# Two normalizations applied on GpSimd in the attention stages, and one wait ahead of the coefficient sum

## What is computed

```python
x = x + 0.5 * ffn(layernorm(x), gate_w, expert_w)
x = x + attn(layernorm(x), Wq, bq, Wk, bk, Wv, bv, Wo, bo)
x = x + 0.5 * ffn(layernorm(x), gate_w, expert_w)

# layernorm: (x - mean) / sqrt(var + 1e-5) over the 1024 features
# ffn:  logits = x @ gate_w.T; top 2 of 8 experts, softmax over the two;
#       out = sum over experts of weight[n, e] * (x @ expert_w[e].T)   (all 8 experts are computed)
# attn: q = f(x Wq + bq), k = f(x Wk + bk), f(z) = exp(-z*z/2); v = x Wv + bv
#       coeff = sum over a head's 64 features of q*k, per token; out = (coeff * v) Wo + bo
```

## Time and profile before

| | us |
|---|---|
| runs shown (2) | 3063.6 and 3078.4, median 3071.0 |
| the profiled execution | 3060.3 |
| its span on the slowest core, first to last instruction | 3058.8 |
| spans of the 8 cores | 3048.6 to 3058.8 |
| one pair of tiles in the steady state | about 355 |

### The profile page before, as it was taken

One profiled execution on the slowest core, in us unless ns is written; L12 is line 12 of the kernel. 1 busy time (PEld: TensorE's weight loads), 2 busy tenths in 40 slices (PEclk: granted clock), 3 DMA queues, 4 the chain that ended last, 5 costly groups with the idle time before them and its releaser, 6 DMA issues.

```text
span 3058.8 us, 58132 instructions; the slowest of 8 cores (3048.6 to 3058.8 us)
## 1 busy us (share of the span) xinstructions
PE 2618.4 (86%) x22240; PEld 2073.3 (68%) x22240; DVE 897.0 (29%) x1920; ACT 526.1 (17%) x1201; POOL 1196.9 (39%) x1059
## 2 busy tenths in 40 slices
PE   0029979998899979998799978999799988999799
PEld 0018757786678857786578856787577865788568
DVE  0012442214411352224432144122522144221530
ACT  0011231103111121112211031111211023110310
POOL 1015215560355405552155603553055512555045
PEclk9999999999999999999999999999999999999999
DMA  9960230104101040103201041011401032010500
GB/s 150 186 174 1 87 108 29 56 1 138 56 29 56 31 164 1 71 14 105 90 29 56 1 153 42 29 56 53 141 16 69 1 111 84 28 43 1 172 22 29
DMA packets 48316, 205.21 MB, mean 67 GB/s; under 512 B 6040, under 2 KB 6040, under 8 KB 42928
## 3 DMA queue, kind: packets, MB, share of 16 engines
q1 hardware_dynamic: 43920, 176.20, 16.8%
q0 software_dynamic: 4128, 25.30, 5.2%
HBM read 201.61 MB, written 25.17 MB: 74 GB/s over the span
## 4 chain that ended last, share of the span: by engine, by line
PE 73%; DVE 10%; DMA 8%; issue 3%; ACT 2%; DVEq 2%; POOL 1%; ACTq 0%; SPq 0%; POOLq 0%
PE P L434 56%; PE P L570 4%; PE P L502 3%; DMA Wexp<-w_exp 3%; DVE yecB L299 2%; PE P L512 2%; PE P L610 2%; DMA Wab<-w_attn 2%; DMA Wab<-w_attn_bf 2%; PE P L252 2%; PE P L224 1%; DVEq L118 1%; DVE yecA L299 1%; DVE SAB L302 1%; DMA w_attn_bf<-Wab 1%
## 5 line engine op out<-in xcount | busy, mean ns | idle before, releaser
L424 POOL TENSOR_TENSOR yecA<-SAA,SCA 128x512 bf16<-128x512 bf16 x512 | 589.5, 1155 | 1301.6 <-ACT SCA L399 873.7
L434 PE MATMUL P<-yecA,Wexp 128*128 128x256 bf16 x8192 | 934.3, 273 | 10.7 <-POOL yecA L424 8.9
L434 PE MATMUL P<-yecB,Wexp 128*128 128x256 bf16 x8192 | 921.1, 273 | 0.0
L434 PEld LDWEIGHTS P<-yecA,Wexp 128*128 128x128 bf16 x8192 | 784.5, 98 | 142.1 <-issue 51.4
L434 PEld LDWEIGHTS P<-yecB,Wexp 128*128 128x128 bf16 x8192 | 790.1, 98 | 118.1 <-issue 27.4
L424 POOL TENSOR_TENSOR yecB<-SAB,SCB 128x512 bf16<-128x512 bf16 x512 | 591.6, 1159 | 386.2 <-PE P L434 380.7
L452 DVE TENSOR_TENSOR XT<-XT,P 128x512 f32<-128x512 f32 x128 | 79.4, 682 | 652.0 <-PE P L434 652.0
L224 PE MATMUL P<-SAA,onescol 128*1 128x256 bf16 x192 | 25.8, 278 | 203.5 <-DVE SAA L211 202.9
L224 PEld LDWEIGHTS P<-SAA,onescol 128*1 128x1 bf16 x192 | 14.5, 84 | 213.0 <-issue 209.1
L502 PE MATMUL P<-SAB,Wab 128*128 128x256 bf16 x512 | 78.6, 305 | 53.6 <-DVE SAB L302 35.2
L244 ACT ACTIVATE yecA<-SAA 128x512 bf16<-128x512 bf16 x96 | 60.4, 629 | 311.8 <-PE P L252 184.4
(11 more groups left out here) (129 smaller groups left out, 1968.9 us busy)
## 6 DMA issues: line engine op xcount, KB each, us to landing
Wab<-w_attn_bf SPq DMA_DIRECT2D x256, 512.0 KB, 4.2
Wexp<-w_exp POOLq DMA_DIRECT2D x8, 2048.0 KB, 49.3
XT<-x_in SPq DMA_DIRECT2D x16, 1024.0 KB, 5.6
x_out<-XT SPq DMA_DIRECT2D x16, 1024.0 KB, 4.2
Wab<-w_attn POOLq DMA_DIRECT2D x16, 512.0 KB, 10.2
w_attn_bf<-Wab SPq DMA_DIRECT2D x16, 512.0 KB, 8.8
id<-c_id POOLq DMA_DIRECT2D x1, 32.0 KB, 2.5
IND<-c_ind POOLq DMA_DIRECT2D x1, 32.0 KB, 2.2
```

What stands on the lines that cost most here:

```text
L424: yd = inc("gp", lambda g, _c=c0, _e=e, _p=pp: g.tensor_mul(yec[:, _p * 2 * T:(_p + 1) * 2 * T].rearrange("p (h n) -> p h n", h=2), sa[:, ...
L434: fn = lambda tt, _e=e, _c=c, _dj=dj, _p=pp, _h=half, _bk=bank, _lo=lo: tt.matmul(_bk[:, _lo:_lo + T], Wexp[:, ((_e * NCH + _c) * D + _dj ...
```

## The change

With `use_gp` set, the four subtracts and four multiplies of the normalization go to POOL's list in place of DVE's, with POOL's semaphore `gq`, POOL's wait for `mrbb`, and POOL's drains. `y_pair` and `y_done` now hold the name of the semaphore beside its value, and the gate and the attention stage wait for that (`wait_tok`). Apart from this, the eight waits of PE for `qk_done[c]`, one ahead of each coefficient matmul, are replaced by one wait for `qk_done[7]` ahead of all eight. No instruction is added or taken away on the engines otherwise, and the steps keep their places.

```diff
@@ ln_chain
-        wait("ve", "se", bcv_done)
+        wait("ve" if not use_gp else "gp", "se", bcv_done)
+        ap_eng, ap_sem = ("gp", "gq") if use_gp else ("ve", "ve")
...
-            op("ve", lambda v, _s=sv, _y=yv: v.tensor_sub(
+            op(ap_eng, lambda E, _s=sv, _y=yv: E.tensor_sub(
                 _y, _s, St.mrbb[:, :].unsqueeze(1).to_broadcast([128, 2, T])))
-            drain("ve")
-            y_pair[cp] = inc("ve", lambda v, _s=sv, _y=yv: v.tensor_mul(
-                _s, _y, St.rbb[:, :].unsqueeze(1).to_broadcast([128, 2, T])), "ve")
-            drain("ve")
+            drain(ap_eng)
+            y_pair[cp] = (ap_sem, inc(ap_eng, lambda E, _s=sv, _y=yv: E.tensor_mul(
+                _s, _y, St.rbb[:, :].unsqueeze(1).to_broadcast([128, 2, T])), ap_sem))
+            drain(ap_eng)
@@ gate_chain
-                wait("pe", "ve", y_pair[c // 2])
+                wait_tok("pe", y_pair[c // 2])
@@ attn_phase
-        wait("pe", "ve", y_done)
+        wait_tok("pe", y_done)
...
+        wait("pe", "ve", qk_done[7])
         coeff_done = None
         for c in range(NCH):
-            wait("pe", "ve", qk_done[c])
             fn = lambda tt, _c=c: tt.matmul(
                 B2[0:16, 0:T], IND[:, _c * 16:(_c + 1) * 16], sc[:, _c * T:(_c + 1) * T],
```

## The result

The changed kernel is slower: its ratio to the kernel before is 1.0289, with a 95% interval of 1.0269 to 1.0310. On 3064 us, what the kernel before takes as a rule in the same series, that is 89 us, where 75 were forecast. Lines from L294 on are one higher than before: L300 and L303 are the subtract and the multiply (before L299, L302), L319 the gate, L503 the query product, L552 the coefficient sum.

A forecast was written before the change was run, and what follows sets the result against it. PE, busy 86%, was taken as the bound, with normalizations on its path. 34.8 + 27.8 + 12.3 = 75 us on 3060.3 gives 3135, on the median 3071.0 gives 3146; it took 3141 us, range 3114 to 3178.

The forecast's parts named there:

- The hole: Between the attention stages PE waits for SAB; POOL ends 4.35 us later than DVE did, 34.8 us in the run.
- The period: Time from one drained POOL normalization operation's start to the next: 1.275 us, with a gap of 0.12.
- The bounds of 1.11 and 1.745: Limits in us per POOL operation: no drain cost from below, 0.59 us idle before each from above.
- The gate: Gate matmuls in the second attention stage wait for SAA; POOL ends 3.48 us later, 27.8 us in the run.
- I add nothing: Longer PE waits between the stages and at L318 meet an already fallen clock, so no extra clock cost.
- Part 2: One wait ahead of all eight coefficient matmuls delays seven of them: 0.77 us a stage, 12.3 us in the run.
- the third rival: Clock falls at the coefficient sum as PE's wait grows to about 2.2 us: 42 us more, 3183; chance 0.07.
- The prediction's own sign of being wrong: Windows after L551, the coefficient sum, showing a clock of 0.5.
- The sum: Whole run: 34.8 + 27.8 + 12.3 = 75 us.
- POOL's floor: POOL's normalization operations start 1.11 us apart despite drains: 56 us in all, 3122, within 2%; chance 0.16.
- POOL at 0.83 us an operation: Fast POOL normalization operations, twice DVE's 0.42 us: would cost 20 us in the run, 3086; chance 0.03.
- The dear drain: POOL idles 0.59 us before each normalization operation, as after PE's release: 53 us more, 3194; chance 0.06.

The follow-up runs named there:

- the runs of either place alone: Kernel before with only LN 2 of B on POOL, ratio 1.0128; kernel before with only LN 3 of A on POOL, ratio 1.0117.
- the fillers: Matmuls nobody reads, run while PE waits: changed kernel with 76 between the stages and 12 ahead of the one wait, 1.0216; kernel before with 36 between the stages, 0.9937.
- The runs with fillers: Unread matmuls ahead of the single qk_done[7] wait: 12 there and 76 between the stages in the changed kernel, 1.0216; seven in the kernel before with that wait, 1.0003.
- Part 2 measured alone, the one wait alone: Kernel before with the single wait for qk_done[7] and every normalization on DVE: ratio 1.0046, 14 us.
- a crowded schedule: Kernel before with LN 2 advanced at every yield from the fifth, both normalizations on POOL: 1.0129; LN 3 advanced too: 1.0032 on POOL, 1.0150 on DVE.
- the one wait with fillers: Kernel before with the single wait for qk_done[7], all on DVE, and seven unread matmuls ahead of that wait: ratio 1.0003.
- all was on DVE one step early: Kernel before, all on DVE, eight waits, LN 2 begun from the second yield and LN 3 from the first: ratio 1.0030.
- LN 2 early on POOL: Kernel before with both normalizations on POOL, eight waits, LN 2 of B advanced at every yield from the fifth: ratio 1.0129.
- LN 3 alone on POOL: Kernel before with only LN 3 of A, carried by the second attention stage, on POOL: ratio 1.0117, 36 us.

## Why the prediction was right, and where it was off

- **The hole.** Forecast 4.35 us more a pair; measured 4.50 in a steady pair (8.89 against 4.39) and 4.98 as a mean of the whole stretch. POOL's start, 0.14 us after ACT, and PE's, 0.36 after POOL, came as forecast. The period was 1.30 us, not 1.275: the gap behind a drain is 0.14 to 0.16 instead of the 0.12 taken. The bounds of 1.11 and 1.745 held it, and it lies where ACT's hand-over pointed.
- **POOL's first use** was not in the sum. In the first pair the first multiply began 2.69 us late, and the hole was 11.44 us. It costs some 2.6 us in the run.
- **The gate.** Forecast 3.48 us; from mrbb to the sixth value block it was 3.65, and the part of the stage grew by 3.67. The difference is the longer period, seven times 0.025. That everything behind the gate moves with it, and that DVE's freedom gives nothing back, is borne out by the runs of either place alone.
- **Clock behind the hole and the gate.** "I add nothing" was right for the hole: the fillers took 2.04 us out of the changed kernel and 2.18 out of the one before. At the gate it came out by a balance that the prediction had not seen. The three value blocks behind the gate take 4.68 us on average instead of 4.33, and the three ahead of it 3.35 instead of 3.96.
- **Part 2, the step that failed, within a sum that held.** The step was that the seven matmuls cost their 0.77 us and the clock nothing, with the third rival, a fall of the clock at the sum, kept apart at 0.07. Together the two stages' parts up to the output blocks grew by 1.82 us in the first (forecast 0.77). The runs with fillers show 0.80 and 0.83 us of it without the clock's part, so the first term was right and about 1 us of clock was missing in the first stage. The rival named the mechanism but mis-sized it. It put 2.6 us on every one of 16 places, from the long hole; behind the short one it was about 1.0 us a pair in the first stage, since the clock fell in some pairs only (18 of 32 on cores 4 to 7) and came back sooner. In the second stage, where the hole is 1.79 us and not 2.2, all 32 had the upper level. The prediction's own sign of being wrong, a clock of 0.5 in a window after L551, did show. Part 2 measured alone is 14 us where 12 were forecast; in the changed kernel, 89 less 71, it is 18.
- **The sum.** Per pair it was 1.71 us short: 1.05 in the first stage ahead of the outputs, 0.63 at outputs and hole, 0.19 at the gate, less 0.13 and 0.03 elsewhere. Times eight that is 14 us, the difference between 75 and 89. The clock at the sum is over half of it, and the range was wide enough to take it in.
- **The rivals.** POOL's floor, a period of 1.11 us, falls with the period of 1.30. POOL at 0.83 us an operation falls with the 1.15 us of every one of the 128 operations. That was the size by the ratio of 1.96 in the Trainium skill's GPSIMD Engine Reference (section 3), and the trace disagrees with it for this operation (1.15 against 0.42 us is 2.7). The dear drain falls with the gap of 0.16.

## What to carry to other kernels

Ask of an operation not which engine has time, but who waits for its result and for how long; an idle engine that takes 2.6 times as long for the same chain (1.30 against 0.50 us a step) is the wrong place when the chain is exposed, and the better one only when it is hidden and the busy engine's queue holds evacuations that PE needs. Moving a chain earlier is not free either: each of its hops stands in an ordered queue, and a crowded schedule turned one wait of 4.4 us into others that summed to as much or more. Count the clock with each wait: where a wait of 2.2 or 3.5 us came up in a new place, the blocks behind it lost another 1.8 to 2.0 us. When a stall can't be removed, its clock dip can: 36 matmuls that nobody reads made the kernel 0.6% faster.

## What the runs showed of the hardware that was not expected

- The length of one standstill of PE does not tell whether the clock falls. At the coefficient sum a hole of 2.2 us was followed by matmuls at or partly at the lower level in 22 of 64 cases (the one wait alone), and holes of 1.2 to 1.4 us in none of 128 (the one wait with fillers). Between the stages, holes of 1.4 to 1.6 us were followed by the lower level in 26 of 64 cases when all was on DVE one step early; with LN 2 early on POOL, holes of up to 2.2 us were in none of 64. In the first of these two the output blocks just ahead had themselves begun at the lower level (above). Whether that is the reason was not tested.
- Behind 36 matmuls with 16 columns of weights, 4.10 us of them in the standing hole, the next eight took 1.03 us, the upper level, in all 64 cases.
- POOL's first multiply of this kind starts 2.69 us after the subtract ahead of it, once in the run, on every core, at whichever place comes first. The wait is for nothing that the profile shows, and multiplies of the FFN (L425) had run on POOL before. From core 7 of the run with LN 3 alone on POOL:

```profile
424.21 1.15 POOL L300 TENSOR_TENSOR yecA<-SAA,mrbbA 128x512 bf16<-128x512 bf16 x1 [83.77 <-ACT mrbbA L291]
428.05 1.15 POOL L303 TENSOR_TENSOR SAA<-yecA,rbbA 128x512 bf16<-128x512 bf16 x1 [2.69 <-issue]
429.36 1.15 POOL L300 TENSOR_TENSOR yecA<-SAA,mrbbA 128x512 bf16<-128x512 bf16 x1 [0.17 <-issue]
```
